# Repeating the first matmul of each projection in layer 1's attention

## The reference

```
x = x + tanh(g_xattn[l]) * attention_l(layernorm(x), ctx)
x = x + tanh(g_ffn[l])   * ffn_l(layernorm(x))          # l = 0..3
```

```
q = x @ Wq.T
k = concat([ctx @ Wk.T, x @ Wk.T]);  v = concat([ctx @ Wv.T, x @ Wv.T])   # 16 heads of width 8
scores = q k / sqrt(8);  attn = [tanh(gate), softmax(scores[..., 1:])]
out = attn @ v                     # rounded to bf16, layernorm with ln_g, ln_b, then @ Wp.T + bp
```

## Time and profile before

| | |
|---|---|
| median of three runs | 1263.54 us |
| the profiled execution | 1273.85 us, its span 1272.1 us |
| TensorE | 956.0 us busy, 75% of the span, 5366 matmuls |
| VectorE | 767.1 us, 60% |
| ScalarE | 570.3 us, 45% |
| GpSimd | 393.6 us, 31% |
| mean granted TensorE clock | 0.848 |

### The profile page before, as it was taken

One profiled execution on the slowest core, in us unless ns is written; L12 is line 12 of the kernel. 1 busy time (PEld: TensorE's weight loads), 2 busy tenths in 40 slices (PEclk: granted clock), 3 DMA queues, 4 the chain that ended last, 5 costly groups with the idle time before them and its releaser, 6 DMA issues. The chain is left out here.

```text
span 1272.1 us, 17163 instructions
## 1 busy us (share of the span) xinstructions
PE 956.0 (75%) x5366; PEld 728.6 (57%) x5366; DVE 767.1 (60%) x1924; ACT 570.3 (45%) x1101; POOL 393.6 (31%) x519
## 2 busy tenths in 40 slices
PE   3798475688788888488888889478867578894766
PEld 2576354566666665256666666357755347773544
DVE  3687665576766775366666656356765424545675
ACT  1576242355555555154555544155643233331553
POOL 2432002123323332146565656333310132220222
PEclk9799577667867877589999999689988689996888
DMA  4000000000000000000000000100000200000001
GB/s 118 1 2 2 1 1 20 1 18 18 18 18 18 18 18 1 0 1 1 1 1 1 1 1 1 36 1 2 2 19 1 58 9 1 1 1 1 1 1 33
DMA packets 25606, 14.12 MB, mean 11 GB/s; under 512 B 10775, under 2 KB 25006, under 8 KB 25390
## 3 DMA queue, kind: packets, MB, share of 16 engines
q1 hardware_dynamic: 25518, 13.03, 3.9%
HBM read 11.98 MB, written 1.05 MB: 10 GB/s over the span
## 5 line engine op out<-in xcount | busy, mean ns | idle before, releaser
L1474 POOL TENSOR_TENSOR L1f_h<-L1f_h,L1f_gb 128x512 f32<-128x512 f32 (+1 forms) x96 | 152.2, 1589 | 117.8 <-DVE L1f_h L1764 97.2
L722 ACT ACTIVATE L_pt<-bank 128x512 f32<-128x512 f32 x224 | 130.3, 597 | 46.6 <-PE bank L608 42.4
L709 ACT ACTIVATE L_part<-bank,L_bias_ca,const 128x256 fp32r<-128x256 f32 x128 | 68.9, 563 | 111.4 <-PE bank L549 111.4
L410 POOL TENSOR_TENSOR L_kc<-L_kc_all,const 128x256 fp32r<-128x256 f32 x96 | 59.0, 618 | 183.0 <-PE bank L608 128.9
L1764 DVE TENSOR_TENSOR L1f_h<-L1f_a,bank 128x512 f32<-128x512 f32 (+1 forms) x96 | 65.5, 682 | 70.7 <-ACT L1f_a L1604 69.9
L1604 ACT ACTIVATE L1f_a<-bank 128x512 f32<-128x512 f32 (+1 forms) x96 | 57.3, 597 | 112.4 <-PE bank L1529 112.4
L1772 DVE TENSOR_TENSOR L1f_h_lo<-L1f_h,L1f_h_hi 128x512 fp32r<-128x512 f32 (+1 forms) x96 | 88.2, 920 | 11.0 <-ACT L1f_h_hi L1617 11.0
L848 DVE TENSOR_REDUCE L_ms<-bank 128x2 f32<-128x512 f32 x128 | 82.8, 687 | 11.7 <-PE bank L570 11.3
L834 DVE SCALAR_TENSOR_TENSOR L_q<-bank,L_bias_c,L_part 128x256 fp32r<-128x256 f32 x96 | 46.2, 481 | 61.2 <-ACT L_part L709 59.9
L846 DVE TENSOR_REDUCE L_mc<-bank 128x8 f32<-128x512 f32 (+1 forms) x96 | 65.4, 682 | 27.7 <-PE bank L563 18.3
L1527 PE MATMUL bank<-L1f_xt_hi,big_hi 128*128 128x512 f32 (+1 forms) x192 | 77.9, 405 | 0.0
(11 more groups left out here) (405 smaller groups left out, 2621.5 us busy)
## 6 DMA issues: line engine op xcount, KB each, us to landing
L_raw<-in_L_ffn_w_dram SPq DMA_DIRECT2D x8, 176.0 KB, 2.3
L_raw<-in_L_ffn_v_dram SPq DMA_DIRECT2D x8, 176.0 KB, 2.4
const<-in_const_dram SPq DMA_DIRECT2D x1, 1036.0 KB, 5.0
x<-in_x_dram SPq DMA_DIRECT2D x2, 512.0 KB
L_raw<-in_L_ffn_w_dram SPq DMA_DIRECT2D x8, 128.0 KB, 2.4
L_mask<-in_mask_Bx1xSxS_ff_dram SPq DMA_DIRECT2D x2, 512.0 KB
out_dram<-x SPq DMA_DIRECT2D x2, 512.0 KB
L_raw<-in_L_ffn_w_dram SPq DMA_DIRECT2D x8, 48.0 KB, 2.5
```

Of the source, the lines that this page charges most:

```text
L709: last = act.activation(part[:, i].bitcast(F32R), b_proj[:, i * S:(i + 1) * S], ACT.Identity, bias=bias_ca[:, i, g:g + 1], scale=pr.c("ak" ...
L722: act.activation(pt[:, g // 2, (g % 2) * NS + i], b_st[(g * NS + i) % 2][:], ACT.Exp, scale=scale).then_inc(sem["exp_done"], 1)
L1474: pool.tensor_tensor(h[0:m, r], h[0:m, r], gb[0:m, gate_slot(c)], ALU.mult).then_inc(sem["h_done"], 1)
```

## The change

In layer 1 alone, the first matmul of each projection is issued three times instead of once. The first two write the same bank half, with start and stop, and the next one overwrites what they wrote.

```diff
                     for i in range(2 if own_keys else 1):
                         o = b_proj[:, i * S:(i + 1) * S]
+                        if own_keys:
+                            for _ in range(2):
+                                pe.matmul(o, wx[:, 2 * i, cols], xt_hi[:], start=True, stop=True)
                         pe.matmul(o, wx[:, 2 * i, cols], xt_hi[:], start=True, stop=False)
                         pe.matmul(o, wx[:, 2 * i, cols], xt_lo[:], start=False, stop=False)
                         last = pe.matmul(o, wx[:, 2 * i + 1, cols], xt_hi[:], start=False, stop=True)
```

## The result

The change makes the kernel slower: ratio 1.0081 to the kernel before, 95% interval 1.0054 to 1.0107 (ten runs of each: medians 1278.39 and 1267.86 us; 0.81% of 1268 is +10.3 us). The forecast was +11.5 us, that is 1275.0 us from the 1263.54 of three runs, in a range of 1261 to 1290. A ratio leaves out runs more than 1.5% above the fastest of the same kernel; since the kernel before spreads evenly over 2%, that takes out up to half of its runs (12 of 23 for e1, e3 and e4), so that a ratio can stand up to 1% higher than one of all runs would, and the table of experiments gives the medians of all runs beside it.

The account below looks back on a forecast made before the run. No single engine bounds the kernel, but a ring of waits between TensorE, ScalarE and VectorE in layer 1's attention. 24.3 - 1.4 - 9.2 - 2.2 = +11.5 us on 1263.5 gives 1275.0 us, range 1261 to 1290.

Parts of the forecast that it names:

- Price (24.3 - 2.2 = 22.1 us): Layer 1's projections: 128 extra matmuls at 0.190 us each make 24.3 us, 2.2 less as half clock shrinks.
- On the path: Projections stand before both VectorE's and TensorE's legs; ScalarE's 51.5 us wait for them would grow by 15 to 24 us.
- Cover (-1.4 us): In 3 of 32 steps, normalising at full clock, VectorE is busy anyway and hides 0.47 us of extras each.
- The clock's return (-9.2 us): Layer 1's attention: 33 us less at half clock, each worth 0.28 us, from longer dense TensorE work.
- five spells that go: Five of 21 clock falls follow denser TensorE pieces; their half-clock spells, 6.5 us each, were taken to vanish.
- Most sit behind VectorE's work: Argument against large returns: most half-clock spells in layer 1's attention follow pieces with VectorE busy, TensorE sparse, no projection.
- B: Rival: the clock gives back about what the matmuls cost, 1263.5 us; chance 0.14 together with extras hidden everywhere.
- C: Rival: padding holds the clock at full through most steps, so faster, down to -24.7 us, 1238.8 us; chance 0.09.
- The stage and what lies behind: Layer 1's attention stretch of 264.3 us would grow by some 12 us; everything behind it as long as before.
- A: Rival: full price of the projection extras, no return from the clock, +22.9 us, 1286.4 us; chance 0.17.
- D: Rival: the extras are hidden everywhere, no measurable change; chance 0.14 together with the clock giving back the cost.

Follow-up runs that it names:

- e1: The change's two extra matmuls before each projection's first, but over 32 of the 128 rows; ratio 1.0665 to the kernel before, median 1344.7 us.
- e3: Four extra matmuls before each projection's first instead of the change's two; ratio 1.0293 to the kernel before, median 1299.2 us.
- e4: Kernel before, with four matmuls added ahead of TensorE's wait for VectorE's second own-key reduction; ratio 0.9948, median 1256.2 us.
- f1_both: The change's two extras per projection added to the kernel with fillers in three waits; ratio 1.0082 to the kernel before, median 1273.5 us.
- e5_waits: Kernel before, with four, six and four filler matmuls in three of TensorE's waits for VectorE, no projection extras; ratio 0.9848, median 1249.3 us.
- e7_behind: Kernel before, with four matmuls a step added behind the value matmuls, before the first own-key scores; ratio 1.0171, median 1290.8 us.
- e8_behind3: Kernel before, with three matmuls a step added behind the value matmuls, before the first own-key scores; ratio 1.0031, median 1275.4 us.

## Why the prediction was right

**Price (24.3 - 2.2 = 22.1 us).** Blocks of the change: 58.8 - 37.4 = 21.4 us. f1_both, where the return is used up, has 23.9; by my estimate 192 x 0.11 x 0.095 = 2.0 us of that are the other projection matmuls, of which more begin at half clock than in e5_waits (0.54 against 0.44). The spacing read from the earlier trace rows is that of the extras, to the last digit, and the weight loads are inside it. The Trainium skill (page "TensorE: Matmul & The Clock Gate", Part 3, "The mechanism") says in one place that weight loads overlap matmuls in flight only where the row groups differ, which the prediction weighed, and in another that a load for the background weight buffer is pulled ahead as well. As a general rule the first does not hold for this case: ten matmuls with all rows and their loads take 1.18 us. Whether the buffer of the second is the reason no run shows. A load that has to wait does appear in e1_rows32, where the rows change between 32 and 128.

**On the path.** ScalarE's wait for the projections grew by 18.8 us, inside the 15 to 24 that were named, and VectorE's by the same.

**Cover (-1.4 us).** It is there, in the normalising steps at full clock (0.8 us to spare at 375.38). In the change's trace five steps have it, since more of them run at full clock. It stays a small term; no run measured it by itself.

**The clock's return (-9.2 us).** Rest of the stage in the two traces: -15.8 us, less the cover; but one trace has the noise of the clock in it. By all runs the clock rose from 0.850 to 0.865, which is about 380 - 344 = 36 us of half clock, x 0.29 = -10 us. The forecast had 33 us x 0.28. The rate was right: over 90 runs time goes with half clock at nearly the same one. The count behind it, five spells that go, was luck. The prediction has it that most falls of the clock follow a sparse piece like those at 403 and 437.3, with TensorE busy 1.3 of 3.0 us, and five a denser one. The trace of before does not bear that out. Of the 24 falls in the stage, 4 have TensorE busy for less than 1.5 us in the 3 us ahead of them, 1 has 1.67, and 19 have 1.9 us or more, like this one:

```profile
341.90:344.90 3.00, 2.47 (x26) 1.91 (x19) 2.97 (x6) 2.24 (x5) 0.14 (x1) 1.00 0.00 0
```

After the change there are 20 falls, 6 of the sparse sort, 2 between and 12 of the dense. So it is the denser sort that went, as the prediction said; but 19 of them could have gone and not 5, seven of them went on balance, and two of the sparse sort came. "Most sit behind VectorE's work" was also what stood against B and C, which by that argument were likelier than the prediction made them. The size held for this dose only. For four extras the same reasoning gave +8 to +22 us and it was +28 to +37, and for matmuls at another place of the step it had the wrong sign.

**The stage and what lies behind.** The stage was to be some 12 us longer; in the one pair of traces it is 5.5, and the +10.3 of all runs is nearer. "As long as before" behind it was right within 3.7 us of 740.

**Rivals.** A (no return, +22.9) is what happens in f1_both, not here. B and C needed half or more of the spells to go: 122 of 162 us are left. D (hidden everywhere) is out, since the waits behind the projections grew by 18.8 us. C's mechanism, activity that releases the clock, is real, and e5_waits shows it: half clock down to 79 us and 19 us gained, but with the matmuls in the waits and not in front of the step.

## What to carry to other kernels

Where an engine's clock depends on its work, as TensorE's does here (0.872 with four fillers in a wait, 0.850 without), a filler has a price and a return, and they are set by different things: the price by what waits behind it, the return by how much half clock it removes, at a rate that two steps of the same kind at either clock give (here 0.28, against 0.29 over 90 runs). Put such work where the engine waits anyway: the same kind of matmul cost 0.8% in front of the projections and gained 1.5% spread over three waits. Read the clock of every run and not of one trace, and try a second dose before believing in a place: here 3 and 4 matmuls a step differed by 1.4%.

## What the runs showed of the hardware

- 128 matmuls over 32 rows left the granted clock as it was (0.852 against 0.850), though TensorE was busy 13.5 us longer; over 128 rows in the same place they raised it to 0.872.
- Passing from 128-row to 32-row matmuls and back cost about 0.59 us a projection at half clock (1.66 against 1.07 us, e1_rows32).
- The kernel before varies from 1253 to 1280 us between runs, and its clock from 0.870 to 0.838 with it.
- The clock's changes and a loop of steps can fall into one pattern that repeats (37.5 us a sample in e7_behind, with four added matmuls a step); with three the trace shows none (32.9 to 36.8 us a sample in e8_behind3).
